# Routing in two token slices with an early scatter, slots used directly as scatter indices, and attention weights kept in PSUM, in a ConvNeXt-MoE plus coordinate-attention kernel on one core

## What is computed

```
# layer 0: depthwise 7x7 conv, LayerNorm over channels, MoE with 8 experts, top 2
x = layernorm(conv7x7_depthwise(input)); xf = x.reshape(T, 128)      # T = 32*56*56 = 100352
topv, topi = top_k(xf @ Wg + bg, 2); wts = softmax(topv)
order = argsort(-wts[:, 0])                    # tokens by priority
cap = int(1.25 * T / 8)                        # 15680 places of each expert
slot = expert*cap + place in order if place < cap, else dropped
y = gelu(buf[slot] @ W1 + b1) @ W2 + b2;  moe = sum of the two y[slot] * gate
out0 = input + x + layer_scale * moe
# layer 1: per image: mean over rows and over columns, 1x1 to 8 channels, h-swish,
#          two 1x1 back to 128 channels, sigmoid -> a_h, a_w
out1 = silu(batchnorm(conv3x3(out0 * a_w * a_h)))
```

## Time and profile before

| | us |
|---|---|
| median of 3 runs | 6246.16 (6243.88 to 6246.7) |
| the profiled execution, its own time | 6245.02 |
| its span in the profile | 6243.3 |
| Route begins, as the stages are cut below | 1109 |
| Route's end begins (L628) | 1326.85 |
| barrier into the expert phase | 1460.4 |
| barrier into the output phase | 3917 |
| POOL busy over the span | 3685.7 (59%) |
| PE matmul busy | 4951.5 (79%) |
| DVE busy | 2408.8 (39%) |

### The profile page before, as it was taken

The page is one execution under the profiler, slowest core; times in us unless marked ns, Lnnn a source line. Parts: engine busy times, 40 slices in busy tenths (PEclk is TensorE's granted clock), DMA queues, the critical chain, the costliest instruction groups (busy, mean ns, idle before and its releaser), DMA issues. The chain is left out here.

```text
span 6243.3 us, 66489 instructions
## 1 busy us (share of the span) xinstructions
PE 4951.5 (79%) x20662; PEld 2758.2 (44%) x20662; DVE 2408.8 (39%) x4673; ACT 1506.8 (24%) x3672; POOL 3685.7 (59%) x3630
## 2 busy tenths in 40 slices
PE   8999999111898797898779878378878788888788
PEld 3566559110454444454444444134444444444444
DVE  0012227993222222222222222455555555555553
ACT  2233337330332232333223323011111111111111
POOL 0000000005787787788778775777777777777773
PEclk9999999555999898999889989689989899999889
DMA  8877769842333333332323322333333222222210
GB/s 169 185 184 195 194 168 284 277 159 79 101 110 103 101 107 94 90 92 87 87 82 95 89 83 59 118 94 99 103 113 93 83 79 81 81 81 85 95 49 32
DMA packets 840400, 711.27 MB, mean 114 GB/s; under 512 B 596073, under 2 KB 681711, under 8 KB 836091
## 3 DMA queue, kind: packets, MB, share of 16 engines
q1 hardware_dynamic: 666362, 466.30, 27.4%
q0 software_dynamic: 109312, 139.69, 8.1%
q10 hardware_dynamic: 64512, 102.79, 4.9%
HBM read 440.11 MB, written 385.75 MB: 132 GB/s over the span
## 5 line engine op out<-in xcount | busy, mean ns | idle before, releaser
L1077 POOL DMA_INDIRECT y_ring<-ye,index_o x1568 | 1733.2, 1105 | 462.3 <-issue 460.4
L754 POOL DMA_INDIRECT xe<-chunk,index x1568 | 1539.6, 982 | 477.3 <-issue 477.3
L1110 PE MATMUL cp<-padded,taps_o 128*128 128x448 f32 x4032 | 1663.6, 571 | 63.7 <-DVE padded L1298 63.7
L1110 PEld LDWEIGHTS cp<-padded,taps_o 128*128 128x128 f32 x4032 | 801.1, 203 | 832.3 <-issue 797.7
L882 ACT ACTIVATE hid<-hid_ps,b_cols 128x448 f32<-128x448 f32 x1120 | 709.3, 633 | 1632.8 <-PE hid_ps L836 1534.6
L844 PE MATMUL y_ps<-hid,w_sb 128*128 128x448 f32 x2240 | 956.5, 573 | 0.4 <-DVE yt L907 0.4
L836 PE MATMUL hid_ps<-xt,w_sb 128*128 128x448 f32 x2240 | 891.5, 541 | 1.5 <-DVE xt L901 1.5
L474 POOL MEMSET zeros<- 98x512 f32 x1 | 0.5, 525 | 1109.2 <-POOLq L105 1109.2
L1253 DVE SCALAR_TENSOR_TENSOR z<-y_ring,gates,z 128x128 f32<-128x128 f32 x1568 | 434.5, 346 | 555.5 <-DMA y_ring<-ye,index_o 538.9
L1176 ACT ACTIVATE outb<-cp,shift,s 128x448 f32<-128x448 f32 x224 | 162.1, 724 | 1912.2 <-PE cp L1110 1912.2
L901 DVE COPY xt<-xt_ps 128x448 f32<-128x448 f32 x280 | 174.9, 625 | 1148.5 <-PE xt_ps L827 1145.9
(11 more groups left out here) (192 smaller groups left out, 3736.7 us busy)
## 6 DMA issues: line engine op xcount, KB each, us to landing
xe<-zeros SPq DMA_DIRECT2D x16, 3920.0 KB
rows_in<-xe SPq DMA_DIRECT2D x280, 224.0 KB, 2.6
ye<-rows_out SPq DMA_DIRECT2D x280, 224.0 KB, 2.3
xin<-in_x_dram SPq DMA_DIRECT2D x256, 196.0 KB
conv<-rows ACTq DMA_DIRECT2D x256, 196.0 KB
pix<-conv SPq DMA_DIRECT2D x224, 224.0 KB, 5.0
xn<-hat SPq DMA_DIRECT2D x112, 448.0 KB, 4.3
chunk<-xn POOLq DMA_DIRECT2D x112, 448.0 KB, 3.8
```

The lines of the kernel that those rows point to most:

```text
L754: pool.indirect_dma_start(out=xe[:, :], out_offset=bass.IndirectOffsetOnAxis(ap=index[ch][:, c, j:j + 1], axis=0), in_=chunk[ch][:, j * C: ...
L1077: pool.indirect_dma_start(out=y[ch][c][:, j * C:(j + 1) * C], out_offset=None, in_=ye[:, :], in_offset=bass.IndirectOffsetOnAxis(ap=index[ ...
L1110: last = pe.matmul(cp[i % 2][:, 0:HB * W], taps[:, t, :], padded[b][:, img, hb * HB + kh:hb * HB + kh + HB, kw:kw + W], start=(t == 0), st ...
```

## The change

- **Two slices.** Route's end runs twice: over the tokens of the first two pairs of images (14 chunks, 98 of 784 tokens in a partition), then over the rest. The running sums of the second slice go on from those of the first (`runs`). To know before the first slice where the kept tokens of an expert start when it has fewer than `cap`, ACT counts the tokens that picked each expert (8 Squares with a sum) and PE sums them.
- **Eight chunks scattered beside the second slice.** The scatter is now a class, `Scatter`, whose buffers live through both phases. In Route, POOL loads five chunks, waits for `zeroed` and for `early_set` (the slots of slice one), and scatters chunks 0 to 7 with no `lull` between. The expert phase goes on with chunk 8.
- **Slots as indices.** The scatter's DMAs take their indices from `slots` itself; `set_index` is gone there. The output phase keeps its own.
- **Operands in PSUM.** In Route the constant 1 of the long scan, the thresholds and the numbers that are added to the counts (`one_ps`, `bound_ps`, `base_ps`) lie in PSUM, and long operations with both inputs in SBUF are cut by expert in the second slice. In the output phase `weigh` lies in PSUM.
- **Room.** `pick` and `junk` are BF16 and the "seen" sums run in them; `signs`, `den`, the `index` tiles and `z` are gone, `z` using the memory of `logits`.

```diff
+EARLY_PAIRS = 2
+EARLY = 8
+class Scatter:
+    RING = 7
+    def load(self, pool, n):
+        g, ch = divmod(n, NCHK)
+        i = n % self.RING
+        pool.dma_start(self.chunk[i][:], self.xn[g * 128:(g + 1) * 128, ch * CHK * C:(ch + 1) * CHK * C]
+                       ).then_inc(self.chunk_in[i], 16)
+    def landed(self, pool, n):
+        turn, i = divmod(n, self.RING)
+        pool.wait_ge(self.scattered[i], (turn + 1) * 2 * CHK * 16)
+        pool.sem_inc(self.chunks_scattered, 1)
+    def put(self, pool, n, limit):
+        turn, i = divmod(n, self.RING)
+        pool.wait_ge(self.chunk_in[i], (turn + 1) * 16)
+        if n + self.RING - 2 < self.chunks:
+            self.load(pool, n + self.RING - 2)
+        for j in range(CHK):
+            for c in range(2):
+                pool.indirect_dma_start(
+                    out=self.xe[:, :],
+                    out_offset=bass.IndirectOffsetOnAxis(ap=self.slots[:, c, n * CHK + j:n * CHK + j + 1], axis=0),
+                    in_=self.chunk[i][:, j * C:(j + 1) * C], in_offset=None,
+                    bounds_check=limit, oob_is_err=False).then_inc(self.scattered[i], 16)
+        if n:
+            self.landed(pool, n - 1)
...
 def route_phase
+    SLICES = ((0, EARLY_PAIRS * NCHK), (EARLY_PAIRS * NCHK, GR))
-        pick = [sb(f"pick{c}", [128, E, J]) for c in range(2)]
+        pick = [sb(f"pick{c}", [128, E, J], BF16) for c in range(2)]
+        bound_ps, one_ps, base_ps = flat_total[:, 16:16 + E], flat_total[:, 32:33], flat_total[:, 64:64 + E * GR]
...
         def _(pool):
+            for n in range(scatter.RING - 2):
+                scatter.load(pool, n)
+            pool.wait_ge(zeroed, 16 * ZD)
+            pool.wait_ge(early_set, 1)
+            for n in range(EARLY):
+                scatter.put(pool, n, limit)
...
         def _(act):
+            act.wait_ge(picked, 1)
+            for e in range(E):
+                last = act.activation(junk[:, e, :], work[:, e, :], ACT.Square, accum_out=picks[:, e:e + 1])
+            last.then_inc(picks_counted, 1)
...
         def _(dve):
-                    do(dve.tensor_tensor(seen[:, e, :], seen[:, e - 1, :], work[:, e, :], ALU.add))
+                    do(dve.tensor_tensor(pick[c][:, e, :], pick[c][:, e - 1, :], junk[:, e, :], ALU.add))
...
+            dve.tensor_copy(bound_ps, bound[:])
+            do(dve.memset(one_ps, 1.0))
+            for n, (g0, g1) in enumerate(SLICES):
+                experts = [(0, E)] if n == 0 else [(e, e + 1) for e in range(E)]
+                def scan_flags(what, k):
+                    do(dve.tensor_tensor_scan(counts[:, 1:E * JS + 1], one_ps.to_broadcast([128, E * JS]),
+                                              flags, 0.0, ALU.mult, ALU.add))
...
+                do(dve.tensor_tensor(flags_e, prio_s, bound_ps.unsqueeze(2).to_broadcast([128, E, JS]), ALU.is_equal))
+                scan_flags("ties", 0)
...
+                do(dve.tensor_tensor(grouped(taken), before_token, over_tokens(from_s), ALU.is_lt))
+                for e0, e1 in experts:
+                    last = dve.tensor_tensor(flags[:, e0 * JS:e1 * JS], flags[:, e0 * JS:e1 * JS], taken[:, e0 * JS:e1 * JS],
+                                             ALU.mult)
...
+                scan_flags("kept", 1)
...
+                for c in range(2):
+                    for e0, e1 in experts:
+                        last = dve.tensor_tensor(prio_s[:, e0:e1], pick[c][:, e0:e1, j0:j0 + JS], flags_e[:, e0:e1], ALU.mult)
+                    do(last)
+                    fold(rel[:, j0:j0 + JS], prio_s, ALU.add, counts, JS, 4 if n else 1)
...
+                if n == 0:
+                    dve.sem_inc(early_set, 1)
...
 def expert_phase, POOL
+            for n in range(EARLY, PR * NCHK):
+                scatter.put(pool, n, limit)
+                if n > EARLY:
+                    pool.wait_ge(rested, n - EARLY)
                 pool.memset(lull[:], 0.0).then_inc(rested, 1)
-                    set_index(n + 1, (ch + 1) % NCHK)
...
 def output_phase
-        z = [sb(f"z{c}", [128, CC]) for c in range(NCHK)]
+        z_ring = logits[:].rearrange("p e j -> p (e j)")
+        z = [z_ring[:, c * CC:(c + 1) * CC] for c in range(NCHK)]
-        weigh = sb("weigh", [C, A])
+        weigh = cpre[:, 384:384 + A]
```

More of the change, by code:

```diff
@@ L394, in _, with __init__, route_phase @@
                 chunk(m)
-def route_phase(nc, s, logits, xe, slots, gates, needed):
+class Scatter:
+    RING = 7
+    def __init__(self, nc, ctx, s, xn, xe, slots):
+        sb = lambda name, shape, dt=F32: ctx.enter_context(nc.sbuf_tensor(name, shape, dt))
+        sem = lambda name: ctx.enter_context(nc.semaphore(name))
+        self.xn, self.xe, self.slots = xn, xe, slots
+        self.chunks = s["PR"] * NCHK
+        self.chunk = [sb(f"chunk{i}", [128, CHK * C]) for i in range(self.RING)]
+        self.chunk_in = [sem(f"chunk_in{i}") for i in range(self.RING)]
+        self.scattered = [sem(f"scattered{i}") for i in range(self.RING)]
+        self.chunks_scattered = sem("chunks_scattered")
+    def load(self, pool, n):
[21 more added lines that the diff above has]
+            self.landed(pool, n - 1)
+def route_phase(nc, s, logits, xe, slots, gates, needed, scatter):
     PR, J, CAP, DROP, TILES = s["PR"], s["J"], s["CAP"], s["DROP"], s["TILES"]
@@ L529, in _, with fold @@
             do = own.done
[L530 to L535, removed]
+            def fold(out, of, op, temp, n, parts=1):
+                half, quarter = (temp[:, a * n:b * n].rearrange("p (e j) -> p e j", j=n) for a, b in ((0, 4), (4, 6)))
+                for i in range(parts):
+                    lo, hi = 4 * i // parts, 4 * (i + 1) // parts
+                    last = dve.tensor_tensor(half[:, lo:hi], of[:, lo:hi, :], of[:, 4 + lo:4 + hi, :], op)
+                do(last)
                 do(dve.tensor_tensor(quarter, half[:, 0:2, :], half[:, 2:4, :], op))
@@ L609, in scan_flags @@
                 for e in range(E):
[L610 to L611 removed]
+                    last = dve.scalar_tensor_tensor(flags_e[:, e, :], prio_s[:, e, :], bound[:, e:e + 1], flags_e[:, e, :],
+                                                    ALU.is_gt, ALU.add)
                 do(last)
[L613 removed]
@@ L658, in expert_phase @@
-def expert_phase(nc, s, xn, xe, ye, slots, needed, ln_beta, W1, b1, W2, b2, layer_scale):
+                scan_flags("kept", 1)
+                if g1 == GR:
+                    kept = runs["kept"][:, :, 1:GR]
+                    do(dve.tensor_tensor(kept, kept, spare[:].unsqueeze(2).to_broadcast([128, E, GR - 1]), ALU.add))
+                    do(dve.tensor_scalar(short[:], kept, tile_end[:, 0:1], None, ALU.is_lt))
+                    do(dve.tensor_reduce(fewer[:], short[:], AX_X, ALU.add))
+                    dve.tensor_scalar(needed_by_tile[:], fewer[:], 1.0, None, ALU.add).then_inc(needed_set, 1)
@@ L667, in expert_phase @@
     AHEAD = 5
-    PER_PAIR = 2 * CHK * 16
+    chunks_scattered = scatter.chunks_scattered
     with ExitStack() as ctx:
@@ L764, in _ @@
-            for g in range(PR):
-                pair(g, g == 0, g == PR - 1)
-            pool.wait_ge(scattered[NCHK - 1], PR * PER_PAIR)
-            pool.sem_inc(chunks_scattered, 1)
+            scatter.landed(pool, PR * NCHK - 1)
         @block.sync
@@ L931, in _, with output_phase @@
             result(end - 1, E - 1, TILES - 1, False)
-def output_phase(nc, s, x, xn, ye, ln_beta, slots, gates, out, p):
+def output_phase(nc, s, x, xn, ye, ln_beta, slots, gates, logits, out, p):
     PR, N = s["PR"], s["N"]
```

204 lines of the change are left out of this document (86 added, 118 removed).

## The result

The changed kernel takes 5991.4 us (median of four runs, 5954.8 to 6006.1) against 6245.0 (6243.3 to 6246.7): a ratio of 0.9585, 95% interval 0.9537 to 0.9633. That is 254 us less; forecast were 280, with the range 5932 to 6040 around them. Two things in these numbers want an explanation. The time is 26 above the forecast (the profiled run, at 6006.06, 41 above), and four runs spread over 51 us where four of before spread over 3.

The account below looks back on a forecast made before the run. POOL was taken to bound the expert and output phases, DVE Route. From 6245.0, minus 137 (expert phase) and 146 (output phase) gives 5962; 2 added for PE and a median 1 higher give 5965 us, range 5932 to 6040.

Parts of the forecast that it names:

- Start of the scatter: In Route, the slots of slice one and the zeros both ready at 1350, so the first scatter goes out at 1351.
- Beside slice two: In Route, DVE needs 123 us for slice two; POOL's eight chunks take 151 plus 14 of holds, ending at 1516.
- the upper end of 39 more: Beside slice two, long DVE operations with one input in PSUM hold POOL's scatters as well: 39 us more.
- Expert phase: First scatter at 1518, then 103 periods of 21.14; the last scatter ends at 3713 instead of 3849.7, -137 us.
- Output phase: With weigh in PSUM the gathers are no longer held under the two passes: -146 us, bounds 0 and 159.
- the further 13 in the forecast's lower end: In the output phase, the gathers' small holds go too: 13 us less than the forecast.
- PE's allowance: 2 us added to the sum for PE being a little later at the last gather.
- Hold by the write: Rival, output phase: the hold follows the write to padded, not the second SBUF input; no gain there, 6111 us; 5%.
- PE as the bound: Rival, output phase: PE takes over as the bound and 102 us come back, 6067 us; 7%.
- POOL starved beside slice two: Rival, Route: nearly every DVE operation holds POOL, the eight chunks take some 110 us more, 6075 us; 4%.
- Dear index: Rival, scatters: reading the index from slots costs from 0.18 us a scatter; at 0.22 it gives 6310 us; 3%.
- It doesn't do what it says: Rival, Route: the early chunks could wait for slice two after all; counted with POOL starved beside slice two.

Follow-up runs that it names:

- late_loads: The changed kernel with POOL's five first chunk loads issued behind its wait for the zeros: 5949.37 us, ratio 0.9513 to the kernel before.
- late_again: The changed kernel with the five chunk loads behind the wait for the zeros, once more on a third chip: 5948.48 us, ratio 0.9517.
- loads_first: The changed kernel with the five chunk loads issued first and landed before the zero fill starts: 6632.62 us, ratio 0.9821, on a slower chip.
- one_load: The kernel with five late loads, but one of them issued at the fill's start again: 6618.45 us, ratio 0.9785, on a slower chip.
- weigh_sbuf: The changed kernel with the attention weights in SBUF again: 6134.6 us, ratio 0.9799 to the kernel before.
- early0: The changed kernel with no chunk scattered in Route, all 112 in the expert phase: 6061.93 us.
- first and third set: Two of three sets of four follow-up kernels, each set on another chip; the kernel before took 6252.8 us in the first and 6251.4 in the third.
- second set's chip: The chip of the second four follow-up kernels, slower for this program: the kernel before took 6759.5 us there.
- late_no_lull: The changed kernel with the five loads late and a lull of 8 elements instead of 3000: 7880 us, ratio 1.167, on a slower chip.
- half_lull: The changed kernel with the five loads late and a lull of 1500 elements instead of 3000: 5819.84 us, ratio 0.9311.
- no_lull_again: The changed kernel with the five loads late and a lull of 8 elements instead of 3000, on a third chip: 5692.17 us, one run.
- third set's chip: The chip of the third four follow-up kernels: the kernel before took 6251.4 us there.
- early14: The changed kernel with the five loads late and all 14 chunks of slice one scattered in Route instead of 8: 5935.11 us, ratio 0.9496.

## Why the prediction was right, and where it was wrong

**Start of the scatter: DVE's part right, the zeros wrong.** The slots of slice one, "1326.85 - 6 + 29 = 1350", were ready at 1347.9; the BF16 sums gave what was taken, 4.17 us for 7.03. The step that failed is the next one: "five chunk loads of 448 KB beside them at some 300 GB/s add 7.5, so 1350 too". The prediction added the bytes and held the rate constant. The rate did not stay: 64 MB from 1111 to 1418 are some 209 GB/s on average, where before they took until 1342.5, 278 GB/s; the zeros landed 68 us later than forecast (1418 for 1350). Shown: with the loads behind the fill (late_loads, late_again) or ahead of it (loads_first), or with a single one beside it (one_load), the fill is as steady as before. In all three kernels with five loads beside it (the changed one, weigh_sbuf, early0) SP's issue takes 250 to 285 us. The runs' spread goes with it: 51 and 49 us where the chunks wait for such a fill, 2 to 16 us in the four kernels with the loads late that were timed in the first and third set, 0.8 us in early0, where nothing waits for it. (Each kernel has one trace, so that the fill of its other runs ended elsewhere is inferred.) Not shown is why the fill stays out of step for 200 us when the five loads are long done.

**Beside slice two: right.** Forecast 165 us for eight chunks; 156.4 are measured (1419.03 to 1575.4): a chunk with no hold takes 18.5 instead of 18.9, and the late start left only the last 47 us of slice two beside them, so the holds came to 9 instead of 14. Where nearly the whole of slice two lies beside the chunks, late_loads has 163 (1349.1 to 1512.1), with some 15 of holds. The hold under two SBUF inputs was there in late_loads (scatters of 2.5 and 2.3 us, many of 1.3 to 1.5), and the upper end of 39 more was not, since PSUM operands hold nothing. The two longest fall under L688 (784 elements, 1.56 us), which reads two SBUF tensors: not everything of that kind was cut to 686 elements. DVE was done with slice two at 1466 (forecast 1474): it began 2 us earlier and took 118 instead of 123.

**Route's end: 68 late, and a wait that had no term.** Behind the last scatter POOL waits 8.8 us at the barrier, in every kernel with early chunks. In early0, where POOL has no scatters out at that point, it passes the barrier 0.5 us after DVE is done. What the 8.8 consist of is not shown: in the changed kernel the DMA engines move nothing more from 2 us behind the last scatter on, so scatters in flight are at most 2 of them. In the sum it cancels here against the eight quick chunks: 68 late at the first scatter, 9 quicker, 9 at the barrier, and 68 late again at the first expert scatter (1586 for 1518).

**Expert phase: right.** First expert scatter to last end is (3766.0 - 1586.0 - 17.7) / 103 = 21.0 for a period of 21.14. The index copy is gone, and a scatter is 8 ns shorter (972 for 980) where 0 to 22 longer were feared. Tail 68 from scatter to barrier, as before. PE caught up, helped by a first tile 33 us behind the barrier instead of 40 or more; its waits for rows fell from 404 to 232 us.

**Output phase: right.** -152.5 for -146, between the bounds 0 and 159. The holds of over 2 us gave 146 of it (147.4 before, 1.7 now; they were 63 gathers, not 66, 62 of them under the passes). The median gather, 997 ns instead of 1004, gave 11. Some 4 came back in shorter holds, 11.2 us between 1.1 and 2 us for 6.6 before; the further 13 in the forecast's lower end, the small holds, did not go. The stage in numbers (columns as above), to set against the earlier trace rows:

```profile
3835.00:6004.00 2169.00, 1764.74 (x5020) 913.02 (x5020) 1241.91 (x2087) 261.07 (x355) 1616.55 (x1688) 0.90 0.29 92
```

**The sum.** +68 start (net, at the first expert scatter), -15 from 103 periods, -6.5 in the output phase, -2 for PE's allowance and -3 behind the last gather (87.9 us to the end for 90.8) give some 41, from 5965 to the profiled 6006.

**The rivals.** *Hold by the write*: refuted by weigh_sbuf. What the Trainium skill tells of a probe and was weighed (SBUF — State Buffer, section Who interferes with whom: `tensor_tensor` did not stall a DMA from GpSimd) doesn't hold here: the trace has TENSOR_TENSOR hold a gather for 4.25 us in weigh_sbuf and for none with one PSUM operand; a TENSOR_TENSOR_SCAN held a scatter for 12.15. The section's other sentence, that two SBUF inputs contend with a GpSimd instruction that reads SBUF, describes all of these rows. *PE as the bound*: refuted on the chip of the changed kernel's profile, POOL waits for issue alone; PE's busy time in the stage is 1765 of 2169. On the second set's chip this rival's sign is there: POOL waits for `tp`, 291 us in one_load. *POOL starved beside slice two*: refuted, 156 and 163 us where it would have been some 275. *Dear index*: refuted, 972 ns. *It doesn't do what it says*: part of it came true in a way not thought of. The early chunks did not wait for slice two, but for the zeros, until DVE had done 70 of its 118 us.

**A theory of mine that fell later.** After late_no_lull I held that the pause between chunks lets the other engines run, on every chip. half_lull and no_lull_again show that it is not so on the third set's chip; on the second set's the lull was taken out, and not varied.

**The versions.** Best with certainty on two chips is late_loads (0.951 and 0.952). On the third set's chip half_lull gives 0.931 and no lull 0.910. The second of these, one run, costs 17% on another chip, so it is not to be recommended; half_lull was not run there, nor was half_lull together with early14.

## What to carry to other kernels

When a wait is moved earlier, everything that it waits for becomes critical, and that which had 120 us of room before has to be priced anew: its end is then no longer "bytes over rate", and small transfers beside it can cost ten times their bytes (75 us for 7.5). Put small loads before or behind a bulk transfer that somebody waits for. If an engine that issues indirect DMAs is the bound, look which operations beside it read two tensors from SBUF, and move one of the operands to PSUM. A pause that looks like waste should be measured on more than one chip before it is taken out.

## What the hardware showed that was not expected

- Five loads of 448 KB (2.3 MB) beside a fill of 64 MB delay its end by some 75 us (1418 for 1342.5), where their bytes are worth 7.5; one load delays it by nothing. The rate then alternates between about 134 and 265 GB/s.
- The same program, with the same times on POOL to a few us until Route's end, took 5692 us on one chip and 7880 on another, where POOL's scatters without a pause left PE 388 us of work in 1900.
- Leaving a block right behind scatters costs 8.8 us at the barrier, though the DMA engines move data for at most 2 of them; without scatters before it, 0.5 (early0).
- Indirect DMAs became 4 to 8 ns shorter at the median (scatters 980 to 972 or 974, gathers 1004 to 997 or 1000, by kernel) with no edit to the instruction but where its index lies, and for the gathers not even that.
